# A recurrent stage of a three-part layer, its exact fp32 products replaced by three rounded ones

## The reference, cut to what matters

```
def step(carry, _):
    xs, vs = carry
    u = jnp.tanh(ctx @ w_ctx + xs @ w_x + b_inl)
    vn = vs + DT * (u - xs - vs)
    xn_ = xs + DT * vn
    return ((xn_, vn), None)
(xs, vs), _ = jax.lax.scan(step, (xs, vs), None, length=8)
```

## Time and profile before

| | |
|---|---|
| median of 3 runs | 894.53 us (893.73 to 896.83) |
| the profiled execution, whole | 893.74 us |
| its span, first to last instruction | 892.0 us |
| TensorE busy (records) | 865.2 us, 97% |
| VectorE busy | 575.7 us, 65% |
| ScalarE busy | 489.6 us, 55% |
| GpSimd busy | 176.2 us, 20% |
| mean granted TensorE clock | 0.998 of full speed |

### The profile page before, as it was taken

How to read it: one execution, slowest core, us unless ns; L and a number is a source line. 1 busy time by engine, 2 the same in 40 slices (tenths; PEclk the granted TensorE clock), 3 DMA queues, 4 the chain that set the end, 5 groups by cost and what they waited for, 6 DMA issues and landing times.

```text
span 892.0 us, 11261 instructions
## 1 busy us (share of the span) xinstructions
PE 865.2 (97%) x3967; PEld 526.4 (59%) x3967; DVE 575.7 (65%) x864; ACT 489.6 (55%) x715; POOL 176.2 (20%) x207
## 2 busy tenths in 40 slices
PE   9999999999999999999999999999899999999998
PEld 4665545545455545544446778774345777777775
DVE  4778757757777426678878774366654566665554
ACT  3536566566566755766657555437657433444332
POOL 8712332323222311000011630000015700000000
PEclk9999999999999999999999999999999999999999
DMA  4314405515524114200000000114656200000000
GB/s 148 67 37 75 85 13 98 96 25 96 108 51 93 31 34 165 96 0 1 0 0 22 1 1 1 35 37 87 137 112 156 67 1 25 1 24 1 1 24 24
DMA packets 21879, 46.28 MB, mean 52 GB/s; under 512 B 7896, under 2 KB 10840, under 8 KB 21440
## 3 DMA queue, kind: packets, MB, share of 16 engines
q1 hardware_dynamic: 19136, 43.17, 21.4%
q10 hardware_dynamic: 2080, 1.27, 0.6%
q0 software_dynamic: 608, 1.12, 0.6%
HBM read 17.04 MB, written 2.29 MB: 22 GB/s over the span
## 4 chain that ended last, share of the span: by engine, by line
PE 84%; DVE 5%; ACT 3%; issue 2%; DMA 2%; POOL 1%; SPq 1%; ACTq 0%; DVEq 0%; POOLq 0%
PE psum L1959 12%; PE psum L1721 9%; PE psum L349 9%; PE psum L350 8%; PE psum L351 8%; PE psum L1760 8%; PE psum L1743 8%; PE psum L1687 3%; PE psum L1662 2%; PE psum L1873 2%; PE psum L1724 2%; PE psum L1647 1%; PE psum L1639 1%; PE psum L1946 1%; PE psum L2162 1%
## 5 line engine op out<-in xcount | busy, mean ns | idle before, releaser
L1171 DVE TENSOR_REDUCE part_max<-psum 128x4 f32<-128x512 f32 x288 | 185.5, 686 | 71.0 <-PE psum L1721 56.4
L867 ACT ACTIVATE prob<-psum 128x1024 f32<-128x1024 f32 (+1 forms) x192 | 145.4, 809 | 85.9 <-PE psum L1743 85.4
L1721 PE MATMUL psum<-k,nat_hi 128*128 128x512 f32 x288 | 119.0, 452 | 2.5 <-ACT nat_lo L814 1.2
L1743 PE MATMUL psum<-q,k 128*128 128x512 f32 (+3 forms) x384 | 96.3, 354 | 0.3 <-ACT prob L867 0.3
L1079 ACT ACTIVATE silu<-psum,wt_bias 128x512 f32<-128x512 f32 x64 | 40.5, 684 | 101.9 <-PE psum L351 93.7
L1721 PEld LDWEIGHTS psum<-k,nat_hi 128*128 128x128 f32 x288 | 50.9, 188 | 62.7 <-issue 50.7
L699 POOL TENSOR_SCALAR_AFFINE_SELECT prob<-prob 128x256 f32<-128x256 f32 x128 | 52.3, 415 | 166.0 <-ACT prob L867 164.8
L1760 PE MATMUL psum<-prob,vq 128*32 128x512 f32 (+3 forms) x768 | 81.8, 498 | 1.3 <-POOL prob L699 1.2
L1743 PEld LDWEIGHTS psum<-q,k 128*128 128x128 f32 x384 | 65.2, 189 | 20.5 <-ACT prob L867 8.6
L1580 DVE TENSOR_TENSOR masked_lo<-masked,masked_hi 128x1024 fp32r<-128x1024 f32 x32 | 41.4, 1295 | 42.1 <-ACT masked_hi L1086 42.1
L349 PE MATMUL psum<-masked_hi,wt_hi 128*128 128x512 f32 x128 | 56.2, 439 | 1.2 <-DVE masked_lo L1580 1.2
(11 more groups left out here) (181 smaller groups left out, 1597.5 us busy)
## 6 DMA issues: line engine op xcount, KB each, us to landing
k<-nat_hi SPq DMA_DIRECT2D x92, 64.0 KB, 2.3
xq<-xq_b SPq DMA_DIRECT2D x36, 128.0 KB
q<-nat_hi SPq DMA_DIRECT2D x32, 128.0 KB, 2.3
wt<-in_wt SPq DMA_DIRECT2D x8, 512.0 KB, 4.0
nrm<-in_xT SPq DMA_DIRECT2D x4, 512.0 KB, 8.8
k<-nat_lo SPq DMA_DIRECT2D x32, 64.0 KB, 2.3
q<-nat_lo SPq DMA_DIRECT2D x16, 128.0 KB, 2.3
nrm<-stage SPq DMA_DIRECT2D x32, 64.0 KB, 2.3
```

What stands on the lines that cost most here:

```text
L867: act.activation(prob[:, s % 2, p, :, q0:CH], psum[:, 2 * p:2 * p + 2, q0:CH], ACT.Exp, scale=SCALE)\
L1171: dve.tensor_reduce(part_max[:].rearrange("q (j p i) k -> q p j i k", j=2, p=2)[:, :, :, i, kt], bank(5 + unit_slot[n, u] % 3).rearrange(" ...
L1721: mm = pe.matmul(heads, rounded(nat_hi[:, m, i * P:(i + 1) * P]), k1[:, qd, :, kt * P:(kt + 1) * P], start=True, stop=i != kt)
L1743: mm = pe.matmul(bank(2 * p + j)[:, q0:CH], k2[:, qd, p, j, kt * P:(kt + 1) * P], q2[:, qd, p, c * CH + q0:(c + 1) * CH], start=True, stop ...
```

## The change

In the recurrence the state and its weights are split. GpSimd makes `wx_hi` and `wx_lo` once. For each of the 28 entries of AGAIN ScalarE copies unit 2c of the new state, rounded, into `y_hi`, VectorE copies unit 2c + 1, and GpSimd subtracts both from the state into `y_lo` (two operations). TensorE then does 12 fp32r matmuls for a chunk of iterations 1 to 7 in place of 4 fp32 ones; iteration 0 stays fp32. Room for the new tiles is borrowed from tiles that are used later, so the load of `x0` on SP's queue waits until the last product of the recurrence.

In self-attention, 53 of the 64 diagonal units lose the mask's matmul. Four `tensor_tensor_reduce` of 128 columns, which add the mask and take the maximum, replace their one reduction on VectorE.

The rest are joints: pieces of layer norm 3 and 4 move by a few places on ScalarE, VectorE and TensorE, `widen` goes from VectorE to GpSimd, `join_heads` and its table move into the feed-forward, the tree weights are loaded and split earlier and in other buffers, and 14 idle matmuls at the start become 12.

```diff
-            sp.wait_ge(ln2.var, ln2.at + NCH)
+            sp.dma_start(wt_bias[:], a["wtb"]).then_inc(wt_bias_in, 16)
+            sp.wait_ge(z_ps, UNITS * NITER)
             sp.dma_start(x0[:], a["xT"]).then_inc(x0_in, 16)
-            sp.dma_start(wt_bias[:], a["wtb"]).then_inc(wt_bias_in, 16)
...
+            pool.wait_ge(wx01_ready, 1)
+            pool.tensor_copy(rounded(wx_hi[:]), wx01).then_inc(wx_set, 1)
+            pool.wait_ge(wx_set, 1)
+            pool.tensor_tensor(rounded(wx_lo[:]), wx01, wx_hi[:], ALU.subtract).then_inc(wx_set, 1)
             pool.memset(xvq[:], 1.0).then_inc(zeros_set, 1)
+            def state_low(n, u):
+                pool.wait_ge(y_high[u % 2], again_at(n, u // 2 * 2 + 1) // 2)
+                pool.tensor_tensor(rounded(y_lo(u)), state(n + 1)[:, u % 2, unit_at(u)], y_hi[:, u, :], ALU.subtract)\
+                    .then_inc(y_low, 1)
+            for n, c in AGAIN:
+                for u in (2 * c, 2 * c + 1):
+                    state_low(n, u)
+            pool.wait_ge(z_ps, UNITS * NITER)
...
+            def high_chunk(n, c):
+                for u in (2 * c,):
+                    act.wait_ge(y_ready, done_at(n, u))
+                    act.activation(rounded(y_hi[:, u, :]), state(n + 1)[:, u % 2, unit_at(u)], ACT.Copy)\
+                        .then_inc(y_high[u % 2], 1)
...
-            for n, c in SCAN[2:]:
+            for (n, c), behind in zip(SCAN[2:], [None] + SCAN[2:]):
                 drive_chunk(n, c)
+                if behind in AGAIN[:-1]:
+                    high_chunk(*behind)
+                if (n, c) == AGAIN[-1]:
+                    high_chunk(n, c)
                 if n < NITER - 1:
                     set_chunk(n, c)
...
             def advance_chunk(n, c):
                 for u in (2 * c, 2 * c + 1):
                     advance(n, u)
+                if n < NITER - 1:
+                    u = 2 * c + 1
+                    dve.wait_ge(y_ready, done_at(n, u))
+                    dve.tensor_copy(rounded(y_hi[:, u, :]), state(n + 1)[:, 1, unit_at(u)]).then_inc(y_high[1], 1)
...
+                pe.wait_ge(wx_set, 2)
+                pe.wait_ge(y_low, again_at(n - 1, 2 * c + 1))
+                pe.wait_ge(z_set, again_at(n - 1, 2 * c + 1))
                 for m in range(KT):
-                    for k in range(KT):
-                        mm = pe.matmul(bank(2 * c + m), wx01[:, k, m * P:(m + 1) * P], state(n)[:, k, cols_of(c)],
-                                       start=False, stop=k == 1, skip_group_check=True)
+                    for part in range(3):
+                        for k in range(KT):
+                            w = (wx_lo if part == 2 else wx_hi)[:, k, m * P:(m + 1) * P]
+                            y = y_lo(2 * c + k) if part == 1 else y_hi[:, 2 * c + k, :]
+                            mm = pe.matmul(bank(2 * c + m), rounded(w), rounded(y), start=False,
+                                           stop=part == 2 and k == 1, skip_group_check=True)
                     mm.then_inc(z_ps, 1)
...
+                if i == kt and not masked_in_psum(n, u):
+                    for p in range(2):
+                        for j in range(2):
+                            at = (2 * p + j) * P
+                            ins = dve.tensor_tensor_reduce(
+                                psum[:, 5 + unit_slot[n, u] % 3, at:at + P],
+                                psum[:, 5 + unit_slot[n, u] % 3, at:at + P], caus_f[:], 1.0, -3e38,
+                                ALU.add, ALU.max, accum_out=part_max[:, 16 * j + 8 * p + i, kt:kt + 1])
+                    ins.then_inc(mx_free, 1)
+                    return
...
-                if n == 5:
+                if n == 3:
                     sp.wait_ge(xq2_in[0], q_loaded(3))
                     load_tree(0)
+                if n == 4:
+                    load_tree(1)
                 if n == 6:
-                    load_tree(1)
-                if n == 7:
                     sp.wait_ge(xq2_in[1], q_loaded(7))
                     load_tree(2)
+                    load_tree(3)
             pack_values(XQUADS - 1)
-            load_tree(3)
...
+            widen(0)
             split_weights(0)
+            widen(1)
+            split_weights(1)
             spread_cross(2)
-            split_weights(1)
...
-            run_on(14)
+            run_on(12)
```

More of the change, by code:

```diff
@@ L75, in with_low, with lent @@
             return sb(name, shape, F32, stack), low
+        def lent(name, shape):
+            with ExitStack() as lent_stack:
+                return sb(name, shape, F32, lent_stack)
         def sem(name):
@@ L197, in layer, with y_lo @@
         wff_hi = sb("wff_hi", [P, KT * FF + FT * D])
+        y_lows[0] = lent("y_lo0", [P, 4, CH])
         tree_hi = sb("tree_hi", [P, 2, KT, CH])
+        def y_lo(u):
+            return y_lows[u // 4][:, u % 4, :]
         xk_raw = stage[:].rearrange("p h n -> p (h n)")[:, 0:KT * 4 * CK]\
@@ L255, in layer @@
         begun = sem("begun")
+        wx_set, y_low = sem("wx_set"), sem("y_low")
+        y_high = [sem(f"y_high{m}") for m in range(KT)]
         xq_ps, xq_hi_s, xq_free, xk_ps, xk_hi_s, xk_free, xv_ps, xv_done = [
@@ L334, in layer, with masked_in_psum @@
                         bank_users.append((qk_raw, qk_at(*_ct) + 1))
+        def masked_in_psum(n, u):
+            return self_units[u][0] == self_units[u][1] and (n == 0 or (n == 1 and u < LEAD))
         def slot_free(at):
@@ L754, in spread_cross, with widen @@
                     .then_inc(xden_in, 16)
+            def widen(i):
+                pool.wait_ge(part_set, 1)
+                pool.wait_ge(xrec, i + 1)
+                pool.tensor_tensor(quot_b[0][:, 1, i, :].rearrange("p (s n) -> p s n", s=HD),
+                                   xrecip[:, i, :].rearrange("p (o n) -> p o n", o=1).to_broadcast([P, HD, SEQ // HD]),
+                                   own_part[:].rearrange("p (s o) -> p s o", o=1).to_broadcast([P, HD, SEQ // HD]),
+                                   ALU.mult).then_inc(xspread, 1)
+            widen(0)
             split_weights(0)
+            widen(1)
+            split_weights(1)
             spread_cross(2)
-            split_weights(1)
             for t in (2, 3):
@@ L996, in _ @@
                         act.activation(hid[:, m, :], bank(ff1_bank(m)), ACT.Gelu, bias=v_("ffb1", m)).then_inc(gelu, 1)
-                    if m > 0:
-                        act.wait_ge(gelu, FT * c + m + 4)
-                        act.activation(rounded(hid_hi[:, m - 1, :]), hid[:, m - 1, :], ACT.Copy).then_inc(hid_h, 1)
+                    if c == 0 and m == 1:
+                        square(ln3)(1)
+                    if c == 0 and m == 2:
+                        deviation(ln3)(1)
+                    for i in hidden_after(c, m):
+                        act.wait_ge(gelu, FT * c + i + 5)
+                        act.activation(rounded(hid_hi[:, i, :]), hid[:, i, :], ACT.Copy).then_inc(hid_h, 1)
                     if m == 6 and c == 0:
@@ L1416, in _ @@
                         third_low((1, 3)[c])
+                    if m == 5 and c == 2:
+                        head_tables()
                     if m == (5, 5, 4, 4)[c]:
@@ L1420, in _ @@
                         xq_low(1, 0)
+                if c == 0:
+                    center(ln3)(3)
                 invert(norm)(nc)
@@ L1507, in _ @@
                     xq_low(2, 0)
-                if g == 9:
-                    invert_cross(1)
-                    widen(1)
                 if g == 10:
@@ L1534, in _ @@
                     xq_low(3, g - 4)
-                if g in (6, 14):
-                    invert_cross({6: 0, 14: 2}[g])
-                if g == 5:
-                    dve.tensor_reduce(own_part[:], ident[:].rearrange("p (h s) -> p s h", s=HD), AX_X, ALU.add)\
-                        .then_inc(part_set, 1)
-                    join_heads()
-                if g == 6:
-                    widen(0)
-                if g in (7, 8, 10):
-                    normalize_part({7: 0, 8: 1, 10: 3}[g])
+                if g in (6, 9, 14):
+                    invert_cross({6: 0, 9: 1, 14: 2}[g])
+                if g in (8, 9, 10):
+                    normalize_part({8: 0, 9: 1, 10: 3}[g])
                 if g == 11:
@@ L1721, in unit @@
                 mm = pe.matmul(heads, rounded(nat_hi[:, m, i * P:(i + 1) * P]), k1[:, qd, :, kt * P:(kt + 1) * P],
-                               start=True, stop=i != kt)
-                if i == kt:
+                               start=True, stop=not masked_in_psum(n, u))
+                if masked_in_psum(n, u):
                     mm = pe.matmul(heads, ident_b[:],
@@ L2038, in _ @@
                         xq_projection(1, 0)
-                    if c == 0 and m == 2:
+                    if c == 0 and m == 4:
                         variance(ln3)(1)
-                    if c == 0 and m == 4:
+                    if c == 0 and m == 6:
                         spread_out(ln3)(1)
```

(6 more changed lines are left out.)

65 lines of the change are left out of this document (35 added, 30 removed).

## The result

The changed kernel takes 943.16 us, the median of 4 runs (942.41 to 944.19), against 895.14 for the kernel before beside it (4 runs, 893.73 to 896.83). The ratio is 1.0534, with a 95% interval of 1.0513 to 1.0556: clearly slower. The profiled execution took 944.19 us, its span is 942.4, and its mean granted clock 0.973.

What follows compares the result with a forecast made beforehand. TensorE was taken to bound the kernel before; in the changed recurrence, VectorE and GpSimd taking turns. 46.8 - 6.5 - 0.7 - 2 - 3.5 = +34.1 on 893.74 gave 927.8, predicted as 929 us, 8-in-10 range 906 to 952.

Steps and rivals of the forecast that it cites:

- narrower range of 915 to 942: Whole kernel: the range of the forecast itself, without the rivals, given the remaining chance of 0.60.
- The recurrence: Recurrence stretch: VectorE's and GpSimd's work passes one after another, 153.6 us in all, 46.8 more than before.
- the turns: Recurrence: VectorE and GpSimd alternate on something shared; a chunk costs 4 x 0.60 + 2 x 1.09 = 4.58 us before the copy.
- The three chunks in hand: Recurrence: three chunks, near 15 us, lie between a low part and its use, against a path of about 9; no latency adds.
- Self-attention and start: Self-attention saves 6.5 us by fewer mask matmuls, at 1.15 us a VectorE unit; two fewer idle matmuls at the start save 0.7.
- The rival in which VectorE bounds this stage: Self-attention: at 1.8 us a unit the 6.5 saved become 10 lost, 945 us; chance 0.08.
- I take little more than half the gain, 6.5: Self-attention: of at most 12.2 us of mask matmuls, 6.5 are kept because VectorE then waits almost nowhere.
- Feed-forward joints: Feed-forward: moving layer norm pieces and splitting weights earlier should give 2 us.
- Cross-attention and trees: Cross-attention to the first trees: moved pieces, earlier weight splits and `widen` under GpSimd's idle time should give 3.5 us.
- The clock rival: Recurrence: TensorE also loses its clock; a chunk takes 5.2 us, up to 5.6 with waits, making 946 us; chance 0.17.
- Costed at nothing: Later x0 load, later key copies, splitting the recurrence's weights on GpSimd and the moved bias load were expected to add nothing.
- No turns taken: Recurrence: GpSimd's subtractions run free beside VectorE, about 2.95 us a chunk, kernel 867 us; chance 0.12.

Runs made afterwards that it cites:

- e1: Changed kernel with the recurrence's 56 low parts made on VectorE, one chunk behind its advances, instead of on GpSimd; 916.31 us, ratio 1.0244.
- e3: Kernel before, plus two GpSimd subtractions of 512 columns per recurrence chunk that nothing there waits for; 917.14 us, ratio 1.0255.
- e8: Changed kernel with GpSimd's low parts also waiting for the chunk's look-backs, so they run beside the next advances; tanh in SBUF; 944.47 us.
- e9: Changed kernel with GpSimd's low parts also waiting for the chunk's look-backs, and the tanh left in PSUM; 928.76 us.
- e5: Kernel before with only the self-attention mask change: VectorE's reducing operation adds the mask instead of a matmul; 889.24 us, ratio 0.9922.
- e7: e4 with the second widening moved ahead of the first tree's weight split in GpSimd's queue; 889.11 us, ratio 0.9914.
- e4: Changed kernel with the recurrence's products back in single fp32 form, no high and low parts; 893.69 us, ratio 0.9978.
- e10: e1 with the second high part also made on ScalarE instead of by VectorE's copy; 905.28 us, ratio 1.0129.
- e6: e4 with cross-attention's two widenings back on VectorE, each right behind its reciprocal; 891.22 us, ratio 0.9942.
- e11: Changed kernel with fp32 recurrence products and cross-attention's tables, widenings and order of normalised parts as in the kernel before; 892.52 us, ratio 0.9967.

## Why the prediction was right or wrong

I forecast 929 with 0.85 for slower; it is 943.16, within the range of 906 to 952 and slower as forecast, but 1 us outside the narrower range of 915 to 942 that the forecast's own mechanism had. By its terms, on the profiled execution (927.8 forecast, 944.19 measured), every one came out worse than taken, and 9.0 of the 16.4 us missed are cross-attention and trees:

- **The recurrence, +46.8 forecast, +51.3 measured. The mechanism was right.** TensorE is busy 73%, where I had said some 60; its clock is at 0.89 there. Chunks are 5.03 us apart, forecast 4.98; e1, e3 and the pair e8 and e9 show that it is the turns. The working was off in points that change little: I let all four VectorE operations take turns, and only two do, but each subtraction stands beside one of them, and that is what counts. The copy lies beside no subtraction and still costs 0.46 a chunk (401.33 - 399.67, less two operations of 0.60; 0.40 was taken), since nothing hides it: 4 x 0.60 + 0.46 + 2 x 1.09 = 5.04. The three chunks in hand lie between a product and its tanh, not between a low part and its product. The missing 4.5 are 2.8 in the stretch from first advance to last look-back (156.4 for 153.6) and 1.7 between it and the feed-forward, on which see the clock below.
- **Self-attention and start, -7.2 forecast, -4.5 measured.** A diagonal unit takes 1.23 us on VectorE from start to start, near the 1.15 taken:

```profile
250.44 0.29 DVE L1243 CUSTOM_DVE_ANT_0 psum<-psum,caus_f 128x128 f32<-128x128 f32 x1
250.64 0.14 DVE L1243 DVE_READ_ACCUMULATOR2_ANT part_max<- 128x1 f32 x1
...
251.67 2.48 DVE L1249 TENSOR_REDUCE part_max<-psum 128x4 f32<-128x512 f32 x4
```

  The rival in which VectorE bounds this stage is refuted. The step that failed is "I take little more than half the gain, 6.5": of 12.2 us of matmuls 4.4 are kept (e5). VectorE is busy 87% in a group now. In e5, up to the recurrence, TensorE is busy 10.0 us less than before (334.2 for 344.2) and idle 5.6 us more. Of its waits the trace names 2.2 us for the masked maxima and 1.8 for the row maxima's last step, which was 0.2. Why 10.0 and not 12.2, and what the rest of the idle time is, stays open.
- **Feed-forward joints, -2 forecast, -1.9 measured, but not shown to be by the joints.** e5 has -1.6 with none of them, so that the number came out is luck.
- **Cross-attention and trees, -3.5 forecast, +5.5 measured (6.5 lost, 1.0 gained). This step was wrong.** The row maxima did gain by it, as I had said: TensorE's waits for them are down to 0.8 us. But "`widen` ... lies on GpSimd under idle time" overlooked what is queued ahead of it: the first tree's split, 3.4 us. e7 wins back 2.4 us by one moved line. The trees' waits for `wt_lo` are down from 2.9 us in all to 1.3, not gone. The 2.6 us for `neg_max` vary from run to run of similar kernels (0.5 in e4, 1.1 in e7).
- **The clock rival, 0.17.** The clock did fall in the recurrence, to 0.89, at no cost to the steady chunks: the look-backs start 5.03 us apart (396.30, 401.33, 406.36) whether a pair of matmuls takes 1.05 us (395.77) or 0.62 (400.31), because TensorE has time to catch up. So the rival's 946 is near 943 by chance. Where TensorE has no time in hand a fall does cost. At the stage's end the last product, which the feed-forward stands behind in TensorE's queue, runs from 516.14 to 521.40 at half the clock, 5.3 us for the 2.8 of a product at the full clock:

```profile
515.00:521.00 6.00, 4.86 (x12) 3.84 (x13) 4.77 (x7) 2.65 (x3) 1.04 (x1) 0.51 0.00 0
```

  In e10 the last product runs at the full clock, and from the last look-back to the feed-forward are 7.7 us, as in the kernel before, not 9.4. That points to the 1.7 missing above, though no run changes the clock alone. In cross-attention half the clock costs 1.7 us in the changed kernel and 4 in e6.
- **Costed at nothing.** GpSimd waited 6.1 us for the late load of x0 (`POOL res L767 <- DMA x<-in_xT`), but nothing waited for what it made of it. So the cost of nothing held.
- **No turns taken, 0.12.** Refuted by the look-backs' 3.45.

Without the three products the rest is a gain: e5 889.24 and e7 889.11 both beat the kernel before by 0.8 to 0.9%, and nothing here tells one from the other, so the mask alone can be all of the gain.

## What to carry to other kernels

An idle engine is not free help: before work is moved to GpSimd, see which VectorE operations will stand beside it and where their inputs lie. If both lie in SBUF, add most of GpSimd's time to VectorE's (here 1.09 us for an operation that takes 1.24 alone); doing that work on VectorE itself can be faster (916 against 943). When an operation goes to the end of another engine's queue, read that queue at that moment, not the engine's busy share.

## What the runs showed of the hardware

- An SBUF operand exchanged for one in PSUM frees a VectorE operation of the turns with GpSimd: with one subtraction beside them two operations take 2.38 us from SBUF alone and 1.27 with one input in PSUM. A copy within SBUF isn't free of them: 1.37 us against 0.43.
- GpSimd's share of a turn wasn't fixed: 1.09 us with two input tiles, 0.85 where both inputs were one tile.
- A masked maximum of 128 columns costs VectorE 0.25 us from start to start with the accumulator's read-out (0.14 long) beside it, so a unit of four costs 1.23 where one maximum of 512 columns costs 0.60.
- The granted clock fell while TensorE still waited: in e11's wait of 5.84 us, up to 644.94, the window from 640 to 645 shows 0.53, and the one behind it 0.50. Waits of 2.02 a chunk in the recurrence gave 0.89 over 90 us. A fall cost nothing where another engine set the beat (steps of 5.03 us at either level), and 4 us in e6's cross-attention, where TensorE did.
